# The decay of one state in eight moved to POOL, y copies moved to ACT, and transfers reordered in a scan kernel

## The chip, the cores and the metric

The kernel runs on one core of a Trainium2 chip. The metric is the device time of one execution in microseconds (us), the median of three runs. Engines: PE (TensorE, matmuls; PEld is its weight load), DVE (VectorE), ACT (ScalarE), POOL (GpSimd), SP (SyncE, which here only issues transfers; SPq is its queue). PSUM has eight banks of 128x512 f32, written by PE.

## The reference

Four residual layers on x of 64 batches, 64 steps and 256 features: two attention layers, then two state space layers. The change touches only the second pair:

```python
xr, gate = jnp.split(x @ W_in.T, 2, axis=-1)            # 512 each
xc = silu(conv4(xr + t_emb) + b_conv)                   # causal, 4 taps, each feature apart
xn = (xc - mu) / jnp.sqrt(var + 1e-05) * ln_g + ln_b
Bm, Cm, dt = jnp.split(xn @ W_xproj.T, 3, axis=-1)      # 16 states
dt = jnp.tanh(dt @ W_dt.T + b_dt) * 0.01
Ad = 1.0 + dt * A
Bd = Bm * jnp.minimum(norm(xn), 1.0)
def step(h, inputs):                                    # 64 steps
    ad, bd, xt, ct = inputs
    h = jnp.clip(h * ad[:, :, None] + bd[:, :, None] * xt[:, None, :], -10.0, 10.0)
    yt = jnp.einsum('bd,bdh->bh', ct, h)
    return (h, yt)
y = ys + D * xn
out = y * silu(gate) @ W_out.T
```

## The kernel before

64 batches are G = 8 groups of 8 batches. A state tile of a group is 128 partitions (8 batches x 16 states) by 512 features. Every engine has its program written out by hand; what orders them is semaphores alone, and each engine and SP's queue keep to the order of their program. A loop over two layers holds for each layer three stages.

**Front.** For each group in turn: input projection and convolution, normalisation, B, C and decay, and x split in three bf16 parts (xh, xmi, xlo; POOL makes xlo, `last_parts`). SP stores all of it to HBM: `store_x` (z, the normalised x), `store_gate` (sg), `store_scan`, which is `store_decay` (C and decay), `store_b` and `store_parts`. DVE may write the next group's z (`centred`) only when the store of the last has landed. After group 4's stores would be due, SP loads the tables of pass 0 (`load_tables`: Ub from nine loads, Cc and At from four each). The last group's small work is spread over the first 24 steps of the scan (`last_group`).

**Scan.** Two passes of four groups (QW = 4, index w), each 64 steps, in CHUNKS of CH = 4 steps; two chunks (h = 0, 1) make one round of the loop over c2. For each step and each w:

- PE writes the input term into PSUM bank w (`inputs`, Uw and the x block xq; a row of Uw holds the constant 10);
- DVE makes q = min(R, 20) - PSUM (L1744); q has two buffers by the step's parity;
- ACT makes R = relu(decay * q + 10) (`clamp`, L897), so that R of a step feeds q of the next: this is the chain of the recurrence;
- PE multiplies q by Wy and the x block by By (`y_of`) and collects y of a chunk in PSUM bank 4 + h.

When a chunk's y is full, DVE copies it to ys (`keep_y`, L1750) and SP stores it. POOL stages a chunk ahead (`stage`): four Uw, one for each w, when PE has used the old ones of that h; the decays Ast when ACT has used them; By and Wy when PE has. All eight x steps that fit into xq are refilled by SP (`load_x`, three loads for two steps), one block for each `y_done`. The tables of pass 1 are loaded at c2 = 6 of pass 0, and POOL waits for them (`tab_in[1]`) before it stages pass 1. At the start, xq's blocks 2 and 3 are loaded after group 6's `store_scan`.

**Post.** For each group PE turns y (L1360), DVE adds D*x and multiplies by the gate (yf, yg), PE multiplies by W_out (L1371, 16 matmuls), DVE adds to X (L1792). yt, xnp and sgp have two buffers; SP loads group g+2 when yg of group g is done, first the two gate tensors (`load_gate`, 2 x 1 MB), then y (`load_y`, two loads of 512 KB). PE's turn waits for all four.

## Time and profile before

| | us |
|---|---|
| runs | 1912.21, 1914.29, 1915.49 |
| median | 1914.29 |
| the profiled execution | 1915.77 |
| its span | 1912.7 |

| stretch of the span | what runs |
|---|---|
| 0 to 563 | attention |
| 563 to 797, 1241 to 1467 | front of each layer |
| 797 to 1155, 1467 to 1823 | scan of each layer |
| 1155 to 1241, 1823 to 1909 | post of each layer |

Over the span PE is busy for 1754.8 us, DVE 1646.0, ACT 1305.5, POOL 642.0. These are means over stages with different limits; how long a stage takes is read from the engine that does not wait in it. In a timeline a row is a run of equal instructions: its start, the time to the end of the last, their number, and in brackets the idle time before with what ended it. The instructions of a run overlap a little, so the pitch of one is the difference of starts by their number, not the mean duration.

### The profile page before, as it was taken

The numbers are of one execution on the slowest core, as the hardware profiler recorded it, in microseconds if no ns is written. First come the engines' busy times: TensorE is split into PE (matmuls) and PEld (weight loads), VectorE is DVE, ScalarE is ACT, GpSimd is POOL, SyncE is SP. The second block draws the span as 40 slices with busy tenths as digits, with TensorE's granted clock in tenths as the row PEclk, the third lists the DMA queues.
The fourth block names the chain that finished last, engine by engine and source line by source line (L and its number), as shares of the span: only waits on it lengthen the run. The fifth ranks groups of instructions, "written<-read, shape, count | busy, mean of one in ns | idle before, by whom it ended". The sixth has DMA issues, their size and how long they took to land.

```text
span 1912.7 us, 46171 instructions
## 1 busy us (share of the span) xinstructions
PE 1754.8 (92%) x15152; PEld 823.4 (43%) x15152; DVE 1646.0 (86%) x2380; ACT 1305.5 (68%) x2166; POOL 642.0 (34%) x591
## 2 busy tenths in 40 slices
PE   7999999999989998789999998899987899899978
PEld 5556566565544554322222224445553222222244
DVE  4788888888877997989999996579989899999965
ACT  3555446464637887789989990068877899899900
POOL 0223133232331111536656540001115466565400
PEclk9999999999999999899989999999998999999999
DMA  3000000000002434545445657624345454456577
GB/s 154 2 1 0 1 2 29 2 1 0 2 1 81 161 120 146 184 139 160 151 135 187 210 160 222 192 79 147 133 147 181 142 159 151 139 183 216 157 225 271
DMA packets 127179, 228.29 MB, mean 119 GB/s; under 512 B 36084, under 2 KB 61812, under 8 KB 118004
## 3 DMA queue, kind: packets, MB, share of 16 engines
q1 hardware_dynamic: 127064, 226.80, 36.0%
q8 instruction: 66, 1.08, 0.2%
q14 instruction: 49, 0.40, 0.1%
HBM read 143.40 MB, written 83.36 MB: 119 GB/s over the span
## 4 chain that ended last, share of the span: by engine, by line
PE 58%; DVE 17%; ACT 10%; issue 7%; DMA 5%; SPq 3%; DVEq 1%; POOL 0%; ACTq 0%; POOLq 0%
PE PS L912 14%; PE PS L1321 9%; PE PS L1304 8%; PE PS L1140 7%; ACT R L897 6%; DVE acc L1598 5%; DVE q L1744 4%; PE PS L978 4%; DMA yt<-y_d 3%; PE PS L1371 2%; PE PS L962 2%; PE PS L989 2%; PE PS L1324 2%; PE PS L937 2%; PE PS L972 1%
## 5 line engine op out<-in xcount | busy, mean ns | idle before, releaser
L897 ACT ACTIVATE R<-q,Ast 128x512 f32<-128x512 f32 x1024 | 637.9, 709 | 48.9 <-DVE q L1744 31.0
L1744 DVE SCALAR_TENSOR_TENSOR q<-R,PS 128x512 f32<-128x512 f32 x1008 | 610.2, 677 | 22.5 <-ACT R L897 11.8
L550 POOL TENSOR_TENSOR Uw<-Ub,rowmask 96x512 bf16<-96x512 bf16 x256 | 339.0, 1357 | 193.3 <-PE PS L1304 180.6
L1304 PE MATMUL PS<-xq,Uw 97*128 97x512 bf16 x1024 | 328.1, 398 | 54.7 <-DVE q L1744 39.1
L1321 PE MATMUL PS<-q,Wy 128*32 128x512 f32 x2016 | 284.3, 618 | 0.8 <-DVE q L1744 0.7
L1140 PE MATMUL PS<-X,Win 128*128 (+1 forms) x512 | 242.2, 614 | 5.7 <-DVEq L1577 2.9
L1304 PEld LDWEIGHTS PS<-xq,Uw 97*128 97x128 bf16 x1024 | 86.2, 98 | 371.2 <-DVE q L1744 318.2
L541 POOL TENSOR_TENSOR xlo<-xr,xmi 128x512 bf16<-128x512 f32 x64 | 73.3, 1167 | 457.4 <-ACT xmi L796 457.4
L912 PE MATMUL PS<-xn,Wl 128*128 128x512 f32 x384 | 183.7, 609 | 0.0
L507 POOL TENSOR_TENSOR ex<-ex,rs 128x1024 f32<-128x1024 f32 x32 | 78.5, 2453 | 201.4 <-DVE rs L1446 201.4
L1598 DVE SCALAR_TENSOR_TENSOR acc<-xp,Wc,acc 128x512 f32<-128x512 f32 x192 | 138.7, 780 | 0.5
L1140 PEld LDWEIGHTS PS<-X,Win 128*128 128x128 f32 x512 | 93.6, 194 | 105.6 <-issue 103.3
L654 ACT ACTIVATE pT<-PS 128x512 f32<-128x512 f32 x128 | 73.7, 596 | 95.3 <-PE PS L978 95.3
L1371 PE MATMUL PS<-yg,Wo 128*128 128x512 f32 x256 | 114.2, 601 | 0.0
L1324 PE MATMUL PS<-xq,By 96*32 96x512 bf16 x1024 | 112.3, 390 | 0.0
L1433 DVE TENSOR_REDUCE mx<-PS 128x32 f32<-128x2048 f32 x32 | 73.2, 2287 | 28.4 <-PE PS L962 28.4
L912 PEld LDWEIGHTS PS<-xn,Wl 128*128 128x128 f32 x384 | 67.2, 192 | 59.2 <-issue 54.6
L606 ACT ACT_TABLE_LOAD x18 | 23.1, 1283 | 98.3 <-DVE X L1792 90.0
L500 POOL TENSOR_TENSOR vsc<-vTd,vs_t 128x1024 f32<-128x1024 f32 x16 | 41.1, 2571 | 142.2 <-ACT vTd L646 142.2
L646 ACT ACTIVATE vTd<-PS 128x1024 f32<-128x1024 f32 x32 | 32.7, 1023 | 74.7 <-PE PS L912 74.7
L978 PE MATMUL PS<-ident,ex 128*128 128x128 f32 x512 | 77.6, 285 | 4.6 <-DVE ex L1450 3.0
L1443 DVE TENSOR_REDUCE sm<-ex 128x32 f32<-128x2048 f32 x32 | 73.1, 2283 | 9.5 <-ACT ex L658 9.5
(147 smaller groups left out, 2671.0 us busy)
## 6 DMA issues: line engine op xcount, KB each, us to landing
xq<-xpart_d SPq DMA_DIRECT2D x384, 192.0 KB
sg_d<-sg SPq DMA_DIRECT2D x16, 1024.0 KB, 4.0
xn_d<-z SPq DMA_DIRECT2D x16, 1024.0 KB, 4.1
y_d<-ys SPq DMA_DIRECT2D x64, 256.0 KB, 3.8
xnp<-xn_d SPq DMA_DIRECT2D x16, 1024.0 KB, 5.4
sgp<-sg_d SPq DMA_DIRECT2D x16, 1024.0 KB, 7.8
yt<-y_d SPq DMA_DIRECT2D x32, 512.0 KB, 9.6
xpart_d<-xh SPq DMA_DIRECT2D x16, 512.0 KB, 2.9
```

The lines of the kernel that those rows point to most:

```text
L507: pl.tensor_tensor(late_half(ex, r), late_half(ex, r), rs[:, r, :].rearrange("p (j e) -> p j e", j=4)[:, :, 4:8] .unsqueeze(3).broadcast_t ...
L550: pl.tensor_tensor(Uw[0:XROWS, h, w, :, :, :], Ub[0:XROWS, w, 0:N, ds(s0, CH)].rearrange("p n t -> p t n").unsqueeze(2).broadcast_to([XROW ...
L897: act.activation(R[:, w, :], q[:, t % 2, w, :], ACT.Relu, scale=Ast[:, h, w, t:t + 1], bias=CLIP).then_inc(ac_r, 1)
L912: mm = pe.matmul(PS[:, bank, :], Wl[l][:, w, c, m * P:(m + 1) * P], rhs[:, c, :], start=(c == 0), stop=(c == HC - 1))
L978: mm = pe.transpose(PS[:, turn_bank[k], j * P:(j + 1) * P], ex[:, k // 4, j, (k % 4) * P:(k % 4 + 1) * P], ident[:, :])
L1140: mm = pe.matmul(PS[:, m % DC, :], Win[:, c, m * P:(m + 1) * P], X[:, ds(g, 1), c, :].rearrange("p a t -> p (a t)"), start=(c == 0), stop= ...
L1304: pe.matmul(PS[:, w, :], Uw[0:KROWS, h, w, t, :, :].rearrange("p b n -> p (b n)"), xq[0:KROWS, hb, w, s8 % XT, :], start=True, stop=True). ...
L1321: pe.matmul(PS[32 * w:32 * w + 32, 4 + h, :], Wy[:, h, w, t * 32:(t + 1) * 32], R[:, w, :] if last else q[:, s8 % 2, w, :], start=(t == 0) ...
L1324: mm = pe.matmul(PS[32 * w:32 * w + 32, 4 + h, :], By[0:XROWS, h, t, w, MID - t * GB:MID + (CH - t) * GB], xq[0:XROWS, hb, w, xt, :], star ...
L1371: mm = pe.matmul(PS[:, 4 + 2 * u + m, :], Wo[:, c, m * P:(m + 1) * P], yg[:, u, c, :], start=(c == 0), stop=(c == DC - 1))
L1598: v.scalar_tensor_tensor(out=tiled(acc[:, m, :]), in0=xp[:, m, :, j:j + S], scalar=Wc[:, m, j:j + 1], in1=tiled(acc[:, m, :]), op0=ALU.mul ...
L1744: v.scalar_tensor_tensor(out=q[:, s8 % 2, w, :], in0=R[:, w, :], scalar=2 * CLIP, in1=PS[:, w, :], op0=ALU.min, op1=ALU.subtract).then_inc ...
```

## The change

1. **Decay of w = 3 on POOL at even steps.** In each chunk, at t = 0 and t = 2, R of w = 3 is made by POOL (`decayed`) as max(decay * q, -10), without the constant 10. For the step after it (odd) the constant row of Uw for w = 3 is 0 (one more memset before the first layer), and DVE takes min(R, 10) there. ACT makes 14 of the 16 R of a chunk, POOL two.
2. **y copies on ACT.** `keep_y` moves from DVE to ACT, after its three R of t = 2.
3. **POOL's staging** is cut in halves, `first_half` (Uw of w 0 and 1, Ast) and `second_half` (Uw of w 2 and 3, By, Wy), with one `decayed` between two halves. Each Uw piece waits for its own predecessor, and PE's step t = 0 waits for each piece by itself instead of for all four. The x parts of the last group are made one at a time. Pass 0 is written out instead of looped.
4. **SP in the front.** The z and gate stores of the fifth group (index 4) go ahead of the table loads; these are issued in four pieces between the stores of groups 4 and 5. The x blocks 2 and 3 of the scan are loaded ahead of `store_b` and `store_parts` of group 6. `store_parts` of the last group moves two steps later.
5. **SP in the post stage.** y of group g+2 is loaded when group g has been turned, ahead of the wait for yg and of the gate loads.

```diff
                     for w in range(QW):
+                        if t == 0:
+                            pe.wait_ge(pl_u, cn * QW + w + 1)
                         pe.wait_ge(dv_q, pi * (QW * S) + n * QW + w + 1)
...
+                        pooled = s8 % 2 == 1 and w == LAST
+                        if pooled:
+                            v.wait_ge(pr_r, pi * (S // 2) + (c2 * 4 + s8 // 2) + 1)
...
-                        v.scalar_tensor_tensor(out=q[:, s8 % 2, w, :], in0=R[:, w, :], scalar=2 * CLIP, in1=PS[:, w, :],
+                        v.scalar_tensor_tensor(out=q[:, s8 % 2, w, :], in0=R[:, w, :], scalar=CLIP if pooled else 2 * CLIP, in1=PS[:, w, :],
...
-                            for w in range(QW):
+                            for w in range(QW - (t + 1) % 2):
                                 act.wait_ge(dv_q, cn * (QW * CH) + QW * t + w + 1 + QW)
...
+                            if t == 2 and (h or before):
+                                keep_y(pi, c2 * 2 + h - 1, 1 - h)
...
+                def decayed(ps, c2, h, t):
+                    cn = chunk_no(ps, c2, h)
+                    pl.wait_ge(pl_a, cn + 1)
+                    pl.wait_ge(dv_q, cn * (QW * CH) + QW * t + LAST + 1 + QW)
+                    alone(pl)
+                    pl.tensor_scalar(R[:, LAST, :], q[:, t % 2, LAST, :], Ast[:, h, LAST, t:t + 1], -CLIP, ALU.mult, ALU.max).then_inc(pr_r, 1)
...
+                for c2 in range(CHUNKS // 2):
+                    more = c2 + 1 < CHUNKS // 2
+                    nxt = (0, c2 + 1) if more else (1, 0)
+                    decayed(0, c2, 0, 0)
+                    if c2:
+                        second_half(0, c2, 1)
...
+                    decayed(0, c2, 0, 2)
...
+                    if not more:
+                        pl.wait_ge(tab_in[1], l * (16 * TABLES) + 16 * TABLES)
+                        alone(pl)
+                    first_half(*nxt, 0)
+                    decayed(0, c2, 1, 0)
+                    second_half(*nxt, 0)
...
+                    decayed(0, c2, 1, 2)
...
+                    first_half(*nxt, 1)
```

How it moves the rows. First SP in the front, around the fifth group of a layer. Before, the tables stand ahead of that group's stores (the loop over groups 4 and 5 begins behind them):

```order
L356 REGISTER_ALU x2
L367 DMA Ub<-bpart_d 8x4x1088 x9
L373 DMA Cc<-cc_d 128x1x64 x4
L373 DMA At<-a_d 128x1x64 x4
L406 UNCONDITIONAL_BRANCH
L406 ISA
L319 ISA
L319 DMA xn_d<-z 128x2048
L314 ISA
L315 ISA
L315 DMA sg_d<-sg 128x2048
```

Now:

```order
L323 ISA
L324 DMA xn_d<-z 128x2048
L319 ISA
L320 DMA sg_d<-sg 128x2048
L361 REGISTER_ALU x3
L372 DMA Ub<-bpart_d 8x4x1088 x3
L328 DMA cc_d<-Cn 4x32x64 x2
L328 DMA a_d<-am 4x32x64 x2
L372 DMA Ub<-bpart_d 8x4x1088 x3
L328 DMA bpart_d<-tvp 4x32x64 x6
L349 DMA xpart_d<-xh 128x4x512
L349 DMA xpart_d<-xmi 128x4x512
```

The store of z (xn_d) and of the gate went ahead of the tables, and the nine loads of Ub stand in threes between the groups' other stores.

POOL at the first chunks. Before, a chunk is staged in one piece, here the first chunk and the start of the second:

```order
L550 TENSOR_TENSOR Uw<-Ub,rowmask 96x512 x4
L554 REGISTER_ALU
L556 COPY Ast<-At 128x16
L557 ISA
L559 TENSOR_TENSOR By<-Ub,rowmask 96x16x8
L563 TENSOR_TENSOR Wy<-Cc,masks 128x4x4x8
L547 ISA
L550 TENSOR_TENSOR Uw<-Ub,rowmask 96x512 x4
L554 REGISTER_ALU
L556 COPY Ast<-At 128x16
```

Now, in the scan's first rounds, from the R of w = 3 at t = 0 of a second chunk (TENSOR_SCALAR) through the half with By and Wy and the next R to the following half:

```order
L597 TENSOR_SCALAR R<-q,Ast 128x512
L567 REGISTER_ALU
L568 TENSOR_TENSOR Uw<-Ub,rowmask 96x512
L567 REGISTER_ALU
L568 TENSOR_TENSOR Uw<-Ub,rowmask 96x512
L582 ISA
L584 TENSOR_TENSOR By<-Ub,rowmask 96x16x8
L588 TENSOR_TENSOR Wy<-Cc,masks 128x4x4x8
L597 TENSOR_SCALAR R<-q,Ast 128x512
L567 ISA
L568 TENSOR_TENSOR Uw<-Ub,rowmask 96x512
L567 REGISTER_ALU
```

Two Uw with By and Wy, or two Uw with Ast, stand between two R; whatever a half waits for, the next R is queued behind.

SP in the post stage, half of a round of its loop. Before:

```order
L396 ISA
L396 DMA xnp<-xn_d 128x2048
L397 DMA sgp<-sg_d 128x2048
L392 ISA
L392 DMA yt<-y_d 64x4x512
L392 ISA
L392 DMA yt<-y_d 64x4x512
```

Now:

```order
L397 ISA
L397 DMA yt<-y_d 64x4x512
L397 ISA
L397 DMA yt<-y_d 64x4x512
L401 ISA
L401 DMA xnp<-xn_d 128x2048
L402 DMA sgp<-sg_d 128x2048
```

The two loads of yt went ahead of the two of the gate, and ahead of the wait for yg.

## Rows read from the trace of the kernel before

**Rows 1.** Windows: busy us per engine, clock, DMA share, GB/s; scan, pass 1.

```profile
996.20:1151.00 154.80, 147.75 (x980) 39.14 (x978) 154.80 (x259) 151.06 (x245) 85.95 (x98) 1.00 0.58 183
```

**Rows 2.** Timeline of DVE in the scan: start us, us, instructions.

```profile
1006.33 9.64 DVE L1744 SCALAR_TENSOR_TENSOR q<-R,PS 128x512 f32<-128x512 f32 x16
1015.89 0.68 DVE L1750 COPY ys<-PS 128x512 f32<-128x512 f32 x1
1016.49 9.64 DVE L1744 SCALAR_TENSOR_TENSOR q<-R,PS 128x512 f32<-128x512 f32 x16
```

**Rows 3.** Timeline of ACT in the scan, one chunk.

```profile
1608.06 9.91 ACT L897 ACTIVATE R<-q,Ast 128x512 f32<-128x512 f32 x16 [0.25 <-DVE q L1744]
```

**Rows 4.** Timeline of PE's weight loads in the scan.

```profile
1003.47 0.10 PEld L1304 LDWEIGHTS PS<-xq,Uw 97*128 97x128 bf16 x1 [0.50 <-DVE q L1744]
```

**Rows 5.** Groups of POOL's instructions: busy us, mean ns, idle before; one memset.

```profile
L550 POOL TENSOR_TENSOR Uw<-Ub,rowmask 96x512 bf16<-96x512 bf16 x256 | 339.0, 1357 | 193.3 <-PE PS L1304 180.6 <-DMA At<-a_d 12.7
...
L541 POOL TENSOR_TENSOR xlo<-xr,xmi 128x512 bf16<-128x512 f32 x64 | 73.3, 1167 | 457.4 <-ACT xmi L796 457.4
...
L563 POOL TENSOR_TENSOR Wy<-Cc,masks 128x128 f32<-128x128 f32 x64 | 26.6, 416 | 0.0
L559 POOL TENSOR_TENSOR By<-Ub,rowmask 96x128 bf16<-96x128 bf16 x64 | 26.4, 412 | 98.6 <-PE PS L1324 98.6
...
L556 POOL COPY Ast<-At 128x16 f32 (+1 forms) x64 | 15.0, 234 | 1.3 <-ACT R L897 1.3
...
570.52 0.95 POOL L528 MEMSET Wy<- 128x1024 f32 x1
```

**Rows 6.** Timelines near the end of pass 0: SP's issue, POOL, DVE.

```profile
967.53 2.48 SPq L373 DMA_DIRECT2D At<-a_d  x4
...
972.18 5.24 POOL L550 TENSOR_TENSOR Uw<-Ub,rowmask 96x512 bf16<-96x512 bf16 x4 [6.40 <-DMA At<-a_d]
...
947.41 0.68 DVE L1750 COPY ys<-PS 128x512 f32<-128x512 f32 x1
```

**Rows 7.** SP's timeline in the front, and DVE's wait in both layers.

```profile
715.57 6.63 SPq L367 DMA_DIRECT2D Ub<-bpart_d  x9
...
727.68 0.36 SPq L319 DMA_DIRECT2D xn_d<-z  x1
...
DVE z L1604 <- DMA xn_d<-z: 11.8, 2, 5.9
```

**Rows 8.** Timelines of DVE in two groups and of POOL beside the second.

```profile
747.87 6.83 DVE L1598 SCALAR_TENSOR_TENSOR acc<-xp,Wc,acc 128x512 f32<-128x512 f32 x10
...
776.70 8.70 DVE L1598 SCALAR_TENSOR_TENSOR acc<-xp,Wc,acc 128x512 f32<-128x512 f32 x10
...
766.36 5.36 POOL L550 TENSOR_TENSOR Uw<-Ub,rowmask 96x512 bf16<-96x512 bf16 x4
```

**Rows 9.** Timelines at the start of each scan: PE in both layers, SP.

```profile
812.00 1.89 PE L1304 MATMUL PS<-xq,Uw 97*128 97x512 bf16 x4 [3.35 <-DMA xq<-xpart_d]
...
1482.02 1.03 PE L1304 MATMUL PS<-xq,Uw 97*128 97x512 bf16 x4 [3.09 <-POOL Uw L550]
...
793.91 1.30 SPq L323 DMA_DIRECT2D a_d<-am  x2
...
802.97 1.11 SPq L377 DMA_DIRECT2D xq<-in_ones  x1
```

**Rows 10.** After the scan: wait in both layers, PE's last turn, three windows.

```profile
PE PS L1360 <- DMA yt<-y_d: 19.2, 8, 6.1
...
1224.85 1.97 PE L1360 MATMUL PS<-ident,yt 128*128 128x128 f32 x16 [1.38 <-DMA yt<-y_d]
...
1182.00:1190.00 8.00, 8.00 (x32) 4.38 (x31) 3.95 (x6) 0.00 (x0) 0.00 (x0) 1.00 1.03 346
...
1201.00:1211.00 10.00, 7.84 (x31) 4.22 (x30) 6.54 (x10) 0.00 (x0) 0.00 (x0) 1.00 1.04 324
1211.00:1225.00 14.00, 12.01 (x41) 5.83 (x40) 8.39 (x11) 0.00 (x0) 0.00 (x0) 1.00 0.88 264
```

More of the change, by code:

```diff
@@ L585, in _ @@
-                pl.wait_ge(sg_st, l * (16 * G) + 16 * G + 16)
-                pl.wait_ge(xf_st, l * (16 * G) + 16 * G + 16)
-                alone(pl)
-                pl.memset(words(pass_tables[1][0]), 0.0).then_inc(tab_zero, 1)
-                with pl.Fori(6, CHUNKS // 2) as c2:
-                    for h in range(2):
-                        stage(0, c2, h)
-                pl.wait_ge(tab_in[1], l * (16 * TABLES) + 16 * TABLES)
-                alone(pl)
-                with pl.Fori(0, CHUNKS // 2) as c2:
-                    for h in range(2):
-                        stage(1, c2, h)
+                    first_half(0, 0, h)
@@ new lines, in _ @@
+                    second_half(0, 0, h)
+                for k in range(TT):
+                    last_part(l * G + G - 2, k)
+                last = l * G + G - 1
+                for c2 in range(CHUNKS // 2):
[4 more added lines that the diff above has]
+                        second_half(0, c2, 1)
+                    if c2 == 3:
+                        last_part(last, 2)
+                    decayed(0, c2, 0, 2)
+                    if c2 == 3:
+                        last_part(last, 3)
+                    if not more:
[4 more added lines that the diff above has]
+                    second_half(*nxt, 0)
+                    if c2 == 2:
+                        last_part(last, 0)
+                    decayed(0, c2, 1, 2)
+                    if c2 == 2:
+                        last_part(last, 1)
+                    if c2 == 4:
+                        pl.wait_ge(xlo_r, l * (G * TT) + G * TT)
+                        pl.wait_ge(xq_st, l * (G * 48) + G * 48 + 48)
+                        pl.wait_ge(sg_st, l * (16 * G) + 16 * G + 16)
+                        pl.wait_ge(xf_st, l * (16 * G) + 16 * G + 16)
+                        alone(pl)
+                        pl.memset(words(pass_tables[1][0]), 0.0).then_inc(tab_zero, 1)
+                    first_half(*nxt, 1)
@@ L884, in last_group, with keep_y, clamp @@
                         middle_part(it, 3)
-                def clamp(pi, c2, first, between=None):
+                def keep_y(pi, ck, h):
+                    act.wait_ge(pe_yq, pi * (2 * S) + ck * (2 * CH) + 2 * CH + USED)
+                    act.wait_ge(y_out[h], pi * (CHUNKS // 2 * 16) + (ck - h) * 8 + 16)
+                    act.activation(ys[:, h, :], PS[:, 4 + h, :], ACT.Copy).then_inc(dv_y, 1)
+                def clamp(pi, c2, first, before, between=None):
                     for h in range(2):
@@ L894, in clamp @@
                                 between(c2 * 8 + h * CH + t)
-                            for w in range(QW):
+                            for w in range(QW - (t + 1) % 2):
                                 act.wait_ge(dv_q, cn * (QW * CH) + QW * t + w + 1 + QW)
```

131 lines of the change are left out of this document (78 added, 53 removed).

## The prediction

> **What bounds the kernel now.** I read the stretches first, then each engine in order of time inside them. In the steady scan VectorE (DVE) is busy for the whole stretch, 154.80 of 154.80 us [rows 1]; the time of a chunk is DVE's. Inside it [rows 2], 16 q instructions start at 1006.33 and the y copy at 1015.89: 9.56 us for 16, so 0.5975 each (the 0.68 of a row is longer than the pitch, since instructions overlap). The copy takes 0.60 more: 1016.49 - 1006.33 = 10.16 us for four steps. The others have room. ScalarE (ACT) needs 9.91 us for its 16 R and then sits idle for 0.25 [rows 3]: pitch (9.91 - 0.71)/15 = 0.613. TensorE (PE) waits 0.50 us in the step for DVE's fourth q [rows 4]. POOL's staging is 4 x 1.357 + 0.234 + 0.412 + 0.416 = 6.49 us of each 10.16 [rows 5]. Outside the scan three places are bound by a transfer, and each is touched by the new order: [rows 7], [rows 9], [rows 10].
>
> **The steady scan: -30.0.** The copy leaves DVE. Per layer there are 32 copies: 5 in the first 24 steps, 10 in the rest of pass 0, 1 early in pass 1 beside other idle time, 15 in the rest of pass 1, 1 at the end. 25 lie in the steady part, so 2 x 25 x 0.60 = 30.0, if nobody else is late. ACT gives two R of a chunk and takes one copy of the same shape, which I count like an R: 15 x 0.613 = 9.2 under 9.56 [rows 3]. The tightest pair of steps has seven R and the copy, 4.9 against 4.78, made good in the next pair, which has seven. PE runs at this pace already within each run of 16 q, still waiting for DVE [rows 4].
>
> POOL decides. Its new instruction (one SBUF input of 128x512 f32, a per-partition scalar, multiply and max) has no row; call it D. Below it stands a POOL memset, 0.95 us for 1024 elements, 0.47 for 512, which reads nothing; above it a subtraction of 128x512 with two inputs, 1.167 [rows 5]. I take 0.7, between them, nearer the one with fewer reads. Latency: D may start after q of w=3 and its result is wanted when DVE has done three more q, 3 x 0.5975 = 1.79 later; with about 0.1 to start and to release, D up to 1.6 fits. Throughput: 2D + 6.49 <= 9.56 gives D <= 1.53. In the half with two Uw, By and Wy, D queues behind 2 x 1.357 + 0.83 = 3.54 of the 4.78 between two D; what it is late may be taken from the 1.79: 2D <= 4.78 + 1.79 - 3.54, D <= 1.51. So any D between the two bounds costs nothing; the staging that it is moved past is due over two us later. The same holds for single release of pieces: PE gets w=0 earlier, where it never waits now.
>
> The Trainium skill (GPSIMD Engine Reference, section 3.1) gives bodies of at most two operations 1.03 cycles an element, an estimate of 0.44 us plus dispatch; no run here shows it, and by it the sum is the same.
>
> **First 24 steps: -3.** Five copies go, the first beside idle time: 4 x 0.60 x 2 = 4.8. POOL's share rises here and DVE's small two-input instructions of the last group can be caught behind it (next part); I take off 0.9 a layer.
>
> **Front: -9.8.** SyncE (SP) now issues 17 table loads (nine for B, four for C, four for the decays) in a row from 715.57, and only at 727.68 the store of z, which DVE awaits for 5.9 us in each layer, 11.8 together [rows 7]. The new order puts that store ahead of the tables. Nothing takes its place: the later table loads go behind each group's stores, and the last eight (about 5 us of issue) end some 8 us before the staging that they release would be late. But they do delay it: POOL's first staging, begun at 766.36 now [rows 8], starts about 775 in a schedule that is 5.9 earlier. Staging costs DVE time where DVE reads two SBUF tensors: ten conv steps take 8.70 beside it and 6.83 without [rows 8]; with the smaller cases the group loses about 3.7 us. Afterwards it meets the chain of small normalisation instructions instead, five with two SBUF inputs. I take one us more than now per layer: 11.8 - 2.0.
>
> The trace shows that DVE waits for POOL instructions there and that q, with one input in PSUM, keeps its pitch beside POOL. The Trainium skill (SBUF — State Buffer, "Who interferes with whom") says so: two SBUF inputs contend with a GpSimd instruction that reads SBUF, one does not; the lock is for the whole instruction. By it D leaves q alone. It speaks against the new place of the staging: five small instructions each behind one Uw.
>
> By rows that rival is 5 x 1.34 = 6.7 against 3.7 now, 3 us a layer instead of my 1, a sum 4 us worse.
>
> **First input blocks: -6.5.** PE waits 3.35 and 3.09 us at step 4 of each layer; the second is put down to POOL, whose pieces had long been staged, so it is the same transfer [rows 9]. SP comes to it at 802.97, after the b and x parts of group 6 and a wait for tvp. They now go behind, so that the load follows the decay store, which ends at 795.2: 7.7 us sooner. I count the two waits; four matmuls after them take 1.89 instead of 1.03 for some steps, which may give two us more.
>
> **A new wait in pass 0: +5.6.** POOL's wait for the tables of pass 1 stood with nothing urgent behind it: 6.40 us of idle [rows 6]. Now D of step 60 is queued behind it. SP issues that block without a gap, so its landing is tied to step 50: 972.18 - 947.41 = 24.8 us. At 2.39 a step, step 60's q ends at 23.9 and D's result is wanted at 25.7. POOL gets it out at 24.8 + 2 x 1.34 + 0.2 + 0.1 + 0.7 = 28.5: 2.8 late, twice. Bounds 1 and 4 each.
>
> **After the scan: -13.** PE stands for y and gate loads for 19.2 us in both layers [rows 10]. y now goes first, 4 us before the gates. But PE waits for both, and the 16 DMA engines are full (shares 1.03 and 1.04 at 346 and 324 GB/s). Six groups of 3.15 MB at the mean, 335 GB/s, need 56.4 us; from about 1161.5, when the last y store can have landed, that ends at 1217.9, where the last turn now begins at 1224.85: 6.5 a layer, 13. Without the bandwidth limit it would be about 20; if the gates land no sooner, 4.
>
> **Sum.** 30.0 + 3 + 9.8 + 6.5 - 5.6 + 13 = 56.7. The profiled execution took 1915.8 (span 1912.7, 3.1 around it), so 1859.1; the median of the runs is 1914.3, 1.5 lower: **1858**. Bounds of the terms: 27 to 30, 0 to 6, 4 to 12, 3 to 8.5, -8 to -2, 4 to 20, together 1842 to 1884.
>
> **Rivals.**
> (a) The y loads bring little, the gates being last anyway: 13 becomes 2 to 4, time 1868. For: full DMA engines. Against: a gap in their work after 1211 (share 0.88) that an earlier issue fills. 14%.
> (b) D takes 1.5 to 2.0. Then POOL sets the chunk, 2D + 6.5: at 1.8 it is 10.1, 27 of the 30 are gone, time 1885. 8%.
> (c) Slower: POOL's arithmetic with two operations and a scalar operand takes over 2.1 us. 27 us come from elsewhere, so the chunk must exceed 9.56 + 57/50 = 10.7. At D = 2.45 it is 11.4: 50 x 1.84 = 92 more, 1950. Nothing in the trace has such a rate (2.3 ns an element is the worst), but nothing shows the instruction. 6%.
> (d) The change does not do what it says: the moved loads make another queue late in the front, and one wait replaces the other. 1870. 4%.
>
> **Numbers.** Forecast 68%, own range 1846 to 1870; the rest as above. The range for 8 in 10 is 1842 to 1884. Under 0.2% (4 us) a measurement can't tell a change. Faster 92%, same 2%, slower 6%.
>
> **What would show it.** DVE's q in unbroken runs across chunks at a pitch of 0.60, a chunk of 9.56, no idle time on POOL's R but for one wait of two to three us near the end of each pass 0; D near 0.7; the z store before the tables and no 5.9 us of DVE idle; no transfer wait at step 4; turns of y with waits below two us and full DMA engines between. Wrong if D exceeds 1.5, if POOL's waits for PE or ACT hold a D back in every chunk, or if the first staging stretches DVE's small instructions to over 1.3 us each.

## The result and the profile of the changed kernel

The changed kernel takes 1945.6 us (median; 1937.7 to 1952.9) against 1913.3 for the kernel before on the same chip: ratio 1.017, 95% interval 1.012 to 1.022. It is slower by 32 us, where 1858 was forecast. The profiled execution took 1941.0, its span 1938.8.

The stages, read from starts in DVE's timeline (first z of the front, first q of the scan, the clamp at the end of a pass, last X of the post), us, layer 1 / layer 2:

| stage | before | changed | difference of both | forecast |
|---|---|---|---|---|
| front (z to q) | 206.0 / 205.4 | 201.8 / 203.0 | -6.7 | -9.8 |
| pass 0 | 183.7 / 183.1 | 192.6 / 192.6 | +18.4 | pass 0 and 1: -33.9 |
| pass 1 | 170.1 / 168.9 | 182.5 / 182.2 | +25.8 | |
| post (clamp to X) | 89.6 / 89.0 | 84.7 / 83.3 | -10.6 | -13 |

What lies between differs by 1 us. So front and post came within 3 us of the forecast here, and the scan missed it by 78 us.

Two of POOL's groups (busy us, mean ns of one, idle before them), and ACT's y copies; the first two answer to [rows 5]:

```profile
L568 POOL TENSOR_TENSOR Uw<-Ub,rowmask 96x512 bf16<-96x512 bf16 x256 | 339.9, 1348 | 37.4 <-DMA At<-a_d 28.4
...
L597 POOL TENSOR_SCALAR R<-q,Ast 128x512 f32<-128x512 f32 x128 | 255.3, 1994 | 96.2 <-DVE q L1825 46.7 <-issue 26.8 <-PE PS L1401 11.1
...
L958 ACT ACTIVATE ys<-PS 128x512 f32<-128x512 f32 x64 | 36.8, 575 | 4.3 <-PE PS L1401 4.3
```

L597 is the new instruction, D: **1.99 us** (128 of them, 1.992 to 2.100), where I took 0.7 and let it reach 1.17. Its 255 us account for the growth of POOL's busy time, 642.0 to 895.0; the staging costs what it did.

DVE in pass 1 (answers to [rows 2]); the times in brackets are idle time and what ended it:

```profile
1033.81 0.69 DVE L1825 SCALAR_TENSOR_TENSOR q<-R,PS 128x512 f32<-128x512 f32 x1 [0.64 <-POOL R L597]
1034.74 4.28 DVE L1825 SCALAR_TENSOR_TENSOR q<-R,PS 128x512 f32<-128x512 f32 x7 [0.24 <-issue]
1039.46 5.02 DVE L1825 SCALAR_TENSOR_TENSOR q<-R,PS 128x512 f32<-128x512 f32 x8 [0.44 <-POOL R L597]
...
1055.85 0.69 DVE L1825 SCALAR_TENSOR_TENSOR q<-R,PS 128x512 f32<-128x512 f32 x1 [0.62 <-POOL R L597]
```

DVE stops at each q of w = 3 in an odd step, and POOL's R ends each stop. From 1033.81 to 1055.85 are two chunks, four pairs of steps of 5.65, 5.53, 5.32 and 5.54 us: 11.02 a chunk, where it was 10.16. POOL in the same pass, a little later:

```profile
1059.47 2.00 POOL L597 TENSOR_SCALAR R<-q,Ast 128x512 f32<-128x512 f32 x1 [0.79 <-DVE q L1825]
1061.54 2.64 POOL L568 TENSOR_TENSOR Uw<-Ub,rowmask 96x512 bf16<-96x512 bf16 x2
1064.15 0.40 POOL L584 TENSOR_TENSOR By<-Ub,rowmask 96x128 bf16<-96x128 bf16 x1
1064.50 0.40 POOL L588 TENSOR_TENSOR Wy<-Cc,masks 128x128 f32<-128x128 f32 x1
1065.00 1.99 POOL L597 TENSOR_SCALAR R<-q,Ast 128x512 f32<-128x512 f32 x1
1067.08 2.64 POOL L568 TENSOR_TENSOR Uw<-Ub,rowmask 96x512 bf16<-96x512 bf16 x2
1069.66 0.20 POOL L577 COPY Ast<-At 128x16 f32 x1
1070.32 1.99 POOL L597 TENSOR_SCALAR R<-q,Ast 128x512 f32<-128x512 f32 x1 [0.46 <-DVE q L1825]
```

Two kinds of step pairs alternate. Between 1059.47 and 1065.00 POOL has no idle time: D, two Uw, By and Wy take 5.53 us for a pair of steps, in which DVE has 4.78 of work. Between 1065.00 and 1070.32 (5.32) POOL waits for DVE (0.46): here it is latency, five q from the one that waited to the one that D reads, then D, then the next q. Once in eight steps, behind the last q of a round of its loop over c2, DVE is idle for 0.24 more and waits for nothing that the profile shows (row 1034.74); that makes the longest pair. ACT is no longer near the bound: it sits idle for 0.38 to 0.45 in the same pairs.

### The profile page after: what moved, and what is told of

Same layout as the page of the kernel before. It is cut to its first block and busy times, and to the rows that moved or that the text cites. A ratio compares the mean times of both kernels' runs of the same rounds, so it can differ in the third digit from the quotient of the medians.

```text
span 1938.8 us, 46236 instructions
## 1 busy us (share of the span) xinstructions
PE 1739.6 (90%) x15152; PEld 815.6 (42%) x15152; DVE 1628.1 (84%) x2316; ACT 1276.8 (66%) x2102; POOL 895.0 (46%) x720
## 5 line engine op out<-in xcount | busy, mean ns | idle before, releaser
L1825 DVE SCALAR_TENSOR_TENSOR q<-R,PS 128x512 f32<-128x512 f32 x1008 | 620.3, 683 | 88.2 <-POOL R L597 63.2
L971 ACT ACTIVATE R<-q,Ast 128x512 f32<-128x512 f32 x896 | 579.5, 712 | 121.9 <-DVE q L1825 100.0
L1381 PE MATMUL PS<-xq,Uw 97*128 97x512 bf16 x1024 | 321.4, 395 | 105.8 <-DVE q L1825 96.9
L597 POOL TENSOR_SCALAR R<-q,Ast 128x512 f32<-128x512 f32 x128 | 255.3, 1994 | 96.2 <-DVE q L1825 46.7
L1381 PEld LDWEIGHTS PS<-xq,Uw 97*128 97x128 bf16 x1024 | 82.1, 97 | 420.0 <-DVE q L1825 379.2
L524 POOL TENSOR_TENSOR ex<-ex,rs 128x1024 f32<-128x1024 f32 x32 | 78.5, 2453 | 201.4 <-DVE rs L1523 201.4
```

The lines of the kernel that those rows point to most:

```text
L524: pl.tensor_tensor(late_half(ex, r), late_half(ex, r), rs[:, r, :].rearrange("p (j e) -> p j e", j=4)[:, :, 4:8] .unsqueeze(3).broadcast_t ...
L597: pl.tensor_scalar(R[:, LAST, :], q[:, t % 2, LAST, :], Ast[:, h, LAST, t:t + 1], -CLIP, ALU.mult, ALU.max).then_inc(pr_r, 1)
L971: act.activation(R[:, w, :], q[:, t % 2, w, :], ACT.Relu, scale=Ast[:, h, w, t:t + 1], bias=CLIP).then_inc(ac_r, 1)
L1381: pe.matmul(PS[:, w, :], Uw[0:KROWS, h, w, t, :, :].rearrange("p b n -> p (b n)"), xq[0:KROWS, hb, w, s8 % XT, :], start=True, stop=True). ...
L1825: v.scalar_tensor_tensor(out=q[:, s8 % 2, w, :], in0=R[:, w, :], scalar=CLIP if pooled else 2 * CLIP, in1=PS[:, w, :], op0=ALU.min, op1=AL ...
```

## Experiments

"The changed kernel" is the one measured above. A chunk's time is read as above, between equal rows of DVE in pass 1. The kernels ran on three chips, so each ratio is to the kernel before on the same chip, whose median was 1912.1, 1915.9 or 1914.4 us; times of kernels from two chips can differ by some 4 us for that alone.

### How much the transfers gave

The kernel before with SP's two new orders (items 4 and 5 of the change, no others).

> The kernel before with SP's two new orders alone (front and post); POOL makes no R, the y copies stay on DVE. Theory 1 (what the changed kernel loses, it loses by POOL's R of 1.99 us, and the transfers gave what its trace shows): front 4.1 + 2.8 us shorter, the two waits at step 4 (3.35 and 3.09) gone, post 4.9 + 5.7 shorter, together 24: 1889 us, steady chunk 10.16 as before. Theory 2 (the post gains only because the scan before it ends late or the y copies moved): post at most 4 shorter in both layers, 1896. Slower than 1905 would say that the transfers are part of the loss.

Measured: 1898.7 us (1897.8 to 1901.4), ratio 0.992 (0.990 to 0.994). The chunk is 10.17, as before. Front 200.2 / 203.4, pass 0 180.6 / 180.6, post 86.9 / 88.5. So the transfers are a gain of 13 us, not a part of the loss; the first steps gave most of what the two waits of [rows 9] held (pass 0 3.2 and 2.5 shorter, of 3.35 and 3.09), the front 5.8 and 2.0, the post only 2.7 and 0.5. That is theory 2's limit of 4 us for the post, 7 below theory 1's 10.6, and most of the 10 by which the expected total was missed.

Then the front order alone; the post keeps gates before y (the edit is against the kernel just measured):

```diff
                     for u in range(2):
-                        sp.wait_ge(po_mm, (l * G + g2 * 2 + u) * DC + DC)
-                        load_y(g2 * 2 + u + 2, u)
                         sp.wait_ge(yg_r, (l * G + g2 * 2 + u) * DC + DC)
                         load_gate(g2 * 2 + u + 2, u)
+                        load_y(g2 * 2 + u + 2, u)
```

> The kernel before with SP's new order in the front and at the first x blocks alone; the post stage loads as before (gates, then y). Theory 1 (of the transfers' 13.4 us the trace puts some 8 to 11 in front and first steps, and 3 in the post): 1903 to 1905, post 89 per layer as before. Theory 2 (the y order is worth what was forecast, 6.5 a layer, and was only disturbed in that run): 1911. Theory 3 (the y order costs as much as it gains): 1898.

Measured: 1902.5 (1895.5 to 1910.6), ratio 0.995 (0.993 to 0.997); post 90.3 / 86.5. The intervals of the two overlap, so what the y order is worth can't be told by the totals: 3.8 us between medians, but only 1.5 when each is taken from the kernel before on its own chip (11.9 against 13.4 saved). The stage itself says a little more, since eleven profiled kernels have the new order unaltered: 83.3 to 89.9, mean of their 22 stages 86.9, against 88.9 for the four stages of this kernel and the one before. That is 2 us a layer, with a spread of 3 either way (the next part shows what goes with it).

### What bounds the post

Transfers as changed, and for the six later groups one quarter of sg (the rest of the gating is left out):

```diff
-                        load_gate(g2 * 2 + u + 2, u)
+                        sp.dma_start(xnp[:, u, :, :], xn_d[ds(g2 * 2 + u + 2, 1)].rearrange("a p c t -> p (a c) t")).then_inc(po_in[u], 16)
+                        sp.dma_start(sgp[:, u, 0:1, :], sg_d[ds(g2 * 2 + u + 2, 1), :, 0:1, :]
+                                     .rearrange("a p c t -> p (a c) t")).then_inc(po_in[u], 16)
```

> Transfers as changed, POOL, ACT and DVE as before, and in the post stage only one quarter of the gate tensor sg is loaded for the six later groups (256 KB instead of 1 MB; the other quarters keep old values, so that part of the gating is left out). Theory 1 (the loads are bound by the rate of the DMA engines; what lands last is sg): 2.4 instead of 3.1 MB a group, at 320 GB/s 7.4 us, under the 8.6 that PE and DVE need; PE's waits of 1 to 2 us at each turn go, post 78 to 80 a layer instead of 87. Theory 2 (bound by the chain of issue and landing of the first tensor, whatever the size): at most 2 shorter.

Measured: 1876.7 (one run), post 76.6 / 76.5, below the 78 to 80 of theory 1. PE's turns in this kernel:

```profile
1159.47 1.96 PE L1373 MATMUL PS<-ident,yt 128*128 128x128 f32 x16 [0.30 <-DMA sgp<-sg_d]
1168.14 1.91 PE L1373 MATMUL PS<-ident,yt 128*128 128x128 f32 x16
```

And in the one with whole gates (the two new orders alone), one turn of layer 1 and one of layer 2:

```profile
1160.81 1.96 PE L1372 MATMUL PS<-ident,yt 128*128 128x128 f32 x16 [1.72 <-DMA sgp<-sg_d]
...
1856.55 3.63 PE L1372 MATMUL PS<-ident,yt 128*128 128x128 f32 x16 [2.67 <-DMA sgp<-sg_d]
```

A window of the kernel with one quarter of sg (busy us of PE, PEld, DVE, ACT, POOL, clock, DMA share, GB/s):

```profile
1160.00:1215.00 55.00, 55.00 (x199) 29.73 (x197) 40.28 (x55) 0.00 (x0) 0.00 (x0) 1.00 0.71 207
```

With fewer bytes PE never stops (55.00 of 55.00 us, DMA share 0.71) and a group takes 8.6; with all bytes each of the six later turns of layer 1 waits 1.0 to 2.4 for sgp. The stage is bound by the transfers, and which tensor is last goes with the order: y in [rows 10], sgp now. In the changed kernel the DMA queue moved 19.1 MB between 1171 and 1235, 298 GB/s at a share of 95%, where I had taken 335 at a full share. The kernel before, over its loads of the post stage in layer 1 (the same columns), and one of its turns there with the granted clock beside it:

```profile
1160.00:1225.00 65.00, 54.25 (x184) 29.05 (x183) 41.61 (x57) 0.00 (x0) 0.00 (x0) 0.95 0.92 291
...
1174.42 3.67 PE L1360 MATMUL PS<-ident,yt 128*128 128x128 f32 x16 [5.88 <-DMA yt<-y_d]
...
1174.00:1178.00 4.00, 3.58 (x17) 3.58 (x18) 2.36 (x4) 0.00 (x0) 0.00 (x0) 0.50 1.01 426
```

It moved 291 GB/s there already; my 335 was the mean of two short windows of [rows 10], and the third, with 264, was left out. Over 1160 to 1215 the kernel with whole gates shows 282 GB/s at a share of 0.89, so the engines are not quite full either. How much of the waits is their rate, and how much that the gate loads are issued only after yg, these runs don't separate.

The last two rows show one more price of these waits. After PE had waited 5.88 us, the turn ran at a granted clock of 0.50 (1.2 GHz) and took 3.67 us instead of 1.96. In the new order the waits are shorter, but some turns are still slow, up to 3.6 us: the one at 1856.55 above, with 0.50 from 1857 to 1860, comes after a wait of 2.67. The slow ones follow waits of 1.92 to 4.60 us; after 2.35 and 2.46 others are not slow. This divides the 22 stages with the new order: the 12 in which one of the six later turns is slow take 87.3 to 89.9 us, the 10 without one 83.3 to 86.9. The changed kernel has none in either layer, the kernel before one in each. No experiment changed the clock alone.

### Is it POOL's R?

The changed kernel with all sixteen R on ACT; copies, halves, unrolled pass and transfers stay:

```diff
-        ACT_TWO = 2 * QW - 1
+        ACT_TWO = 2 * QW
...
-                        pooled = s8 % 2 == 1 and w == LAST
+                        pooled = False
...
-                            for w in range(QW - (t + 1) % 2):
+                            for w in range(QW):
```

> The changed kernel with all sixteen R of a chunk on ACT again (constant 10 in every step); y copies on ACT, staging in halves and transfers as changed. Theory 1 (POOL's R sets the chunk of 11.0): the chunk becomes ACT's 17 x 0.613 = 10.42 us, 0.26 above the kernel before over 50 chunks (13 us), less some 3 us in the first 24 steps; with the transfers' 24 us off, 1899. DVE waits for ACT, not for POOL. Theory 2 (the y copies on ACT, the halves or the unrolled pass cost it): the chunk stays above 10.8 and the time above 1930.

Measured: 1905.2 (1900.4 to 1913.6), ratio 0.996 (0.994 to 0.998); chunk 10.29:

```profile
1034.28 9.84 DVE L1821 SCALAR_TENSOR_TENSOR q<-R,PS 128x512 f32<-128x512 f32 x16 [0.42 <-ACT R L967]
...
1054.85 9.83 DVE L1821 SCALAR_TENSOR_TENSOR q<-R,PS 128x512 f32<-128x512 f32 x16 [0.43 <-ACT R L967]
```

ACT's row of this kernel shows the copy's real price: 16 R from 1023.08 to the copy at 1032.88 are 0.6125 each, and the next R starts 0.48 after the copy, at 1033.36.

```profile
1023.08 9.92 ACT L967 ACTIVATE R<-q,Ast 128x512 f32<-128x512 f32 x16
1032.88 0.60 ACT L954 ACTIVATE ys<-PS 128x512 f32<-128x512 f32 x1
1033.36 9.92 ACT L967 ACTIVATE R<-q,Ast 128x512 f32<-128x512 f32 x16
```

16 x 0.6125 + 0.48 = 10.28, the chunk. (1899 was expected; the front's last group, 34.3 in both layers, and the post, 88.9 and 87.5, stayed longer.) So the slowness comes with POOL's R, as theory 1 said: the copies, the halves and the unrolled pass are all still there. And ACT with the copy but without help is slower than DVE with it (10.29 against 10.16).

Then the copies back on DVE, two R on POOL:

```diff
-                            if t == 2 and (h or before):
-                                keep_y(pi, c2 * 2 + h - 1, 1 - h)
...
                         step(pi, c2, s8, first)
+                        if s8 == 2 and before:
+                            keep_y(pi, c2 * 2 - 1, 1)
+                        if s8 == 6:
+                            keep_y(pi, c2 * 2, 0)
```

> The changed kernel with the y copies back on DVE (at steps 2 and 6, as before); two R on POOL and all else as changed. Theory 1 (with D = 1.99 DVE waits for POOL in each pair of steps, and the copy falls into that wait): steady chunk 11.0 to 11.2 as with the copies on ACT, total within 6 us of the changed kernel's. Theory 2 (the copy's 0.60 adds to the wait): chunk 11.6, 1970.

Measured: 1949.6 (1947.4 to 1952.2), ratio 1.019 (1.016 to 1.022), the same as the changed kernel's.

```profile
1026.75 3.08 DVE L1817 SCALAR_TENSOR_TENSOR q<-R,PS 128x512 f32<-128x512 f32 x5 [0.44 <-POOL R L597]
1029.75 0.68 DVE L1823 COPY ys<-PS 128x512 f32<-128x512 f32 x1
1030.35 2.62 DVE L1817 SCALAR_TENSOR_TENSOR q<-R,PS 128x512 f32<-128x512 f32 x4
...
1048.80 3.08 DVE L1817 SCALAR_TENSOR_TENSOR q<-R,PS 128x512 f32<-128x512 f32 x5 [0.44 <-POOL R L597]
```

(1048.80 - 1026.75) / 2 = 11.03. The copies fall into time in which DVE would wait anyway: moving them off DVE, for which the 30 us stood in the sum, gained nothing at this D.

### Why is D 1.99?

Three kernels, each with another form of the one instruction and everything else as changed (one operation; scalar by value; product). The first and the third leave out the lower bound of -10, the second puts 0.99 in place of the decay:

```diff
-pl.tensor_scalar(R[:, LAST, :], q[:, t % 2, LAST, :], Ast[:, h, LAST, t:t + 1], -CLIP, ALU.mult, ALU.max).then_inc(pr_r, 1)
+pl.tensor_scalar(R[:, LAST, :], q[:, t % 2, LAST, :], Ast[:, h, LAST, t:t + 1], None, ALU.mult).then_inc(pr_r, 1)
+pl.tensor_scalar(R[:, LAST, :], q[:, t % 2, LAST, :], 0.99, -CLIP, ALU.mult, ALU.max).then_inc(pr_r, 1)
+pl.tensor_tensor(R[:, LAST, :], q[:, t % 2, LAST, :], Ast[:, h, LAST, t:t + 1].broadcast_to([P, 512]), ALU.mult).then_inc(pr_r, 1)
```

> The changed kernel with POOL's R as one operation with the same scalar pointer (decay x q); the lower bound of -10 is left out. If each of the two operations costs its share, D is about 1.0 to 1.2; if the form with a scalar has one rate whatever it computes, D stays 1.99. Time 1870 to 1885 in the first case, 1940 in the second.

> The changed kernel with POOL's R as 0.99 x q and the lower bound, both scalars given by value instead of the decay read from Ast (the decay of w = 3 at even steps is left out). It asks whether the read of a scalar per partition makes the 1.99. If so, D falls to 1.1 to 1.3 and the time below 1890; if the form with two operations and scalars has its rate wherever they come from, D stays 1.99 and the time 1940.

> The changed kernel with POOL's R as one product of two tensors (q and the decay repeated along the row), without the lower bound of -10, which is left out: it asks what the form with two operations and a scalar costs. Theory A (a product costs what the subtraction xlo costs, 1.17 us): D 1.17 to 1.2, inside the room of three q; POOL 2 x 1.25 + 6.25 = 8.8 a chunk; DVE runs unbroken at 0.5975, chunk 9.56 to 9.7, and the total is near what was forecast for the whole change; with the transfers' 13 (instead of 29) and the copies' place: 1866 to 1880. Theory B (the read or the f32 output sets the rate): D stays 1.9 to 2.0, 1940.

The group of the instruction (busy us, mean ns of one, idle before) with one operation:

```profile
L597 POOL TENSOR_SCALAR R<-q,Ast 128x512 f32<-128x512 f32 x128 | 200.8, 1569 | 100.6 <-DVE q L1825 52.8 <-issue 30.8 <-PE PS L1401 11.4
```

With the scalar by value:

```profile
L597 POOL TENSOR_SCALAR R<-q 128x512 f32<-128x512 f32 x128 | 245.8, 1920 | 96.1 <-DVE q L1825 46.3 <-issue 27.1 <-PE PS L1401 11.9
```

As a product:

```profile
L597 POOL TENSOR_TENSOR R<-q,Ast 128x512 f32<-128x512 f32 x128 | 133.0, 1039 | 144.9 <-DVE q L1825 80.6 <-issue 48.3 <-PE PS L1401 10.6
```

DVE in pass 1 of the product form (the row is cut off by the end of the view):

```profile
1035.62 31.00 DVE L1825 SCALAR_TENSOR_TENSOR q<-R,PS 128x512 f32<-128x512 f32 x51 [0.39 <-PE PS L1381]
```

| form | D (median) | chunk | time | runs |
|---|---|---|---|---|
| two operations, scalar from Ast | 1.99 | 11.02 | 1945.6 | 4 |
| two operations, scalar by value | 1.92 | 10.85 | 1934.0 | 1 |
| one operation, scalar from Ast | 1.57 | 9.98 | 1888.8 | 1 |
| product of two tensors | 1.04 | 9.7 | 1874.5 (1867.7 to 1878.8) | 4 |

So the read of the decay costs 0.07, the second operation 0.43, and the form with scalars by itself, even with one operation, half as much again as a product with two tensor inputs (of which the second repeats one value along the row; the subtraction with two whole inputs, 1.167, is below it too). The 1.57 lies between the two values expected for one operation, so neither of its theories holds; the form by value went as its second, the product as theory A. That the form with fewer reads is the slower one is the opposite of what I assumed when I leaned to the memset. Why the form with a scalar is slow no run shows. The forecast's other terms can now be seen at nearly the pace that they were made for. The ratio of the product form is 0.979 (0.975 to 0.982), and its scans take 676.9 us against 705.8 before and 750.0 in the changed kernel. Of the 78 us by which the scan missed the forecast, 73 come back with this one instruction.

DVE near the end of pass 0 in the product form:

```profile
963.63 3.08 DVE L1825 SCALAR_TENSOR_TENSOR q<-R,PS 128x512 f32<-128x512 f32 x5 [1.96 <-POOL R L597]
967.40 2.48 DVE L1825 SCALAR_TENSOR_TENSOR q<-R,PS 128x512 f32<-128x512 f32 x4 [0.70 <-PE PS L1381]
```

POOL at the same place:

```profile
959.85 2.62 POOL L568 TENSOR_TENSOR Uw<-Ub,rowmask 96x512 bf16<-96x512 bf16 x2 [3.60 <-PE PS L1381]
...
962.56 1.03 POOL L597 TENSOR_TENSOR R<-q,Ast 128x512 f32<-128x512 f32 x1
```

SP's last issue of that block of tables:

```profile
955.67 2.48 SPq L378 DMA_DIRECT2D At<-a_d  x4
```

This is the new wait for the tables of pass 1: POOL idle for 3.60 before the staging, D behind it (the profile names a matmul of PE as the releaser; POOL waits there for the tables and for PE, and PE had run on without a stop), DVE late by 1.96. The loads of the decays are issued until 958.15 and the wait ends 1.7 after that. I had put 2.8, bounds 1 and 4. In the changed kernel the same wait of POOL is 0.61 and DVE's stop there the usual 0.65, because POOL comes late by itself: one price hid the other.

### Latency or load?

If two bounds alternate, taking one away leaves the other. In the changed kernel, w = 3 is taken before w = 2 in every even step by PE, DVE and ACT, so that five q lie between the q that D reads and the one that wants its R, instead of three:

```diff
+        turn_of = lambda t: (0, 1, 3, 2) if t % 2 == 0 else (0, 1, 2, 3)
...
-                    for w in range(QW):
+                    for pos, w in enumerate(turn_of(s8 % CH)):
```

> The changed kernel with w = 3 taken before w = 2 in every even step (t = 0 and 2), nothing else. It takes latency away and leaves POOL's load. Theory 1 (both bind in turn: 5.31 by latency, 5.53 by load): the latency half goes, the load stays, 2 x (1.99 + 0.08) + 5.25 + 0.2 + 0.8 = 10.4 to 10.6 a chunk instead of 11.0, time 1912 to 1925. Theory 2 (latency alone): 9.6 to 9.9, below 1880. Theory 3 (load alone): 11.0 and 1940 stay.

Measured: 1934.4 (1928.7 to 1936.3), ratio 1.010 (1.007 to 1.013), 9 above the end of theory 1's range.

```profile
1032.07 0.69 DVE L1826 SCALAR_TENSOR_TENSOR q<-R,PS 128x512 f32<-128x512 f32 x1 [0.47 <-POOL R L598]
...
1042.65 10.03 DVE L1826 SCALAR_TENSOR_TENSOR q<-R,PS 128x512 f32<-128x512 f32 x16 [0.32 <-POOL R L598]
1053.12 0.69 DVE L1826 SCALAR_TENSOR_TENSOR q<-R,PS 128x512 f32<-128x512 f32 x1 [0.44 <-POOL R L598]
```

(1053.12 - 1032.07) / 2 = 10.53, inside the 10.4 to 10.6 of theory 1. Without the latency the load is left. The time misses by what lies outside the scan: the scans are 18 us shorter than the changed kernel's (732.1 against 750.0), the post 8.5 longer (176.5 against 168.0), as that stage varies (a later turn is slow in both layers here, in none of the changed kernel's).

Now the other way: one R of sixteen on POOL (t = 0), the staging of the next chunk whole behind it, so that the load fits and the latency stays.

```diff
-                            for w in range(QW - (t + 1) % 2):
+                            for w in range(QW - (t == 0)):
...
-                        pooled = s8 % 2 == 1 and w == LAST
+                        pooled = s8 % CH == 1 and w == LAST
...
+                with pl.Fori(0, CHUNKS // 2 - 1) as c2:
+                    decayed(1, c2, 0)
+                    stage(1, c2, 1)
+                    decayed(1, c2, 1)
+                    stage(1, c2 + 1, 0)
```

> One of sixteen R of a chunk on POOL (w = 3 at t = 0) and fifteen on ACT, then the whole staging of the next chunk behind it; y copies on ACT, transfers as changed. Theory 1 (latency of 1.99 us against three q of DVE, and POOL's sum): POOL has 1.99 + 6.49 = 8.5 us of work in a chunk, so only the latency stays: DVE idles 0.44 once a chunk, 9.56 + 0.44 = 10.0, against 9.81 for ACT's 16; 0.16 below the kernel before over 50 chunks, 8 us, and 3 in the first steps: 1878. Theory 2 (a hand-over from and to POOL costs more than its duration, whatever the load): idle of 0.8 or more each, chunk 10.4, 1900.

Measured: 1904.6 (1904.5 to 1908.4), ratio 0.996 (0.994 to 0.998); a miss of 27 us.

```profile
1039.85 9.71 DVE L1799 SCALAR_TENSOR_TENSOR q<-R,PS 128x512 f32<-128x512 f32 x16 [0.44 <-POOL R L592]
1050.00 9.80 DVE L1799 SCALAR_TENSOR_TENSOR q<-R,PS 128x512 f32<-128x512 f32 x16 [0.44 <-POOL R L592]
1060.24 1.88 DVE L1799 SCALAR_TENSOR_TENSOR q<-R,PS 128x512 f32<-128x512 f32 x3 [0.44 <-POOL R L592]
```

The idle time is the 0.44 expected, but the chunk is 10.15 and 10.24. Start to start the late q costs 1.12 instead of 0.60, which is 0.52; and one q in the next step comes 0.15 late in the longer of the two, after PE. PE had waited for the late q and still has the 8 matmuls of q and Wy to do in that step; that this keeps it from making the time up is a reading, not tested. A stop of 0.44 costs 0.59 to 0.68. The rest of the miss is in the transfers (1898.7, where 1889 was the base) and in the last group of the front.

### A kernel that beats both

One R on POOL, w = 3 before w = 2 at t = 0 only, and ACT's copy of y in the gap that the missing R leaves there, one chunk later; SP stores it accordingly.

```diff
+        turn_of = lambda t: (0, 1, 3, 2) if t == 0 else (0, 1, 2, 3)
...
-                            if t == 2 and (h or before):
-                                keep_y(pi, c2 * 2 + h - 1, 1 - h)
+                                if t == 0 and w == 1 and before:
+                                    keep_y(pi, c2 * 2 + h - 2, h)
```

> One R of sixteen on POOL as in the run with one per chunk (chunk 10.19 there), but at t = 0 every engine takes w = 3 before w = 2, so that five q of DVE instead of three lie between the q that POOL reads and the q that wants its R; and the y copy of ACT stands in the gap that the missing R leaves at t = 0, one chunk later than before (two chunks after its own). Transfers as changed. Theory 1 (the loss of a lone R is latency, 2.06 needed against 1.79): room becomes 2.39 + 0.6 = 2.99 from start to start against 0.68 + 0.08 + 1.99 + 0.06 = 2.8, POOL has 8.4 us of work in a chunk, DVE idles for nobody, chunk 9.6 to 9.7 (ACT: 15 x 0.613 + 0.48 = 9.68); 50 x 0.5 below the transfers alone (1898.7): 1872 to 1878. Theory 2 (a hand-over to POOL costs whatever the room, or ACT falls behind): idle of 0.3 or more a chunk stays, 1890 to 1900.

Measured: 1891.6 (1885.9 to 1896.6), ratio 0.987 (0.984 to 0.990), 14 above theory 1's range. The waits for POOL are gone, but the chunk is 9.97, not 9.65:

```profile
1040.36 19.77 DVE L1802 SCALAR_TENSOR_TENSOR q<-R,PS 128x512 f32<-128x512 f32 x32 [0.16 <-PE PS L1357]
1060.29 1.88 DVE L1802 SCALAR_TENSOR_TENSOR q<-R,PS 128x512 f32<-128x512 f32 x3 [0.16 <-PE PS L1357]
```

32 q take 19.93. Each pair of steps holds one late q (0.77 to 0.84 after the last instead of 0.60), put down to PE; ACT is busy for 59.91 of 60 us there and PE for 56.90. Theory 2's "or ACT falls behind" fits that, its hand-over cost does not; which of the two engines holds the last 0.3 us is open.

Last, the same with the staging of the second chunk moved from the front behind POOL's first R:

```diff
-                for h in range(2):
-                    stage(0, 0, h)
+                stage(0, 0, 0)
...
                     decayed(0, c2, 0)
-                    if c2:
-                        stage(0, c2, 1)
+                    stage(0, c2, 1)
```

> The kernel with one R on POOL and w = 3 ahead of w = 2 at t = 0 (1891.6, front 201.8 and 203.2 us from the first z to the first q), with the staging of the second chunk moved behind POOL's first R, so that one chunk's staging instead of two stands beside the front's last group. Theory 1 (the front lost 3 to 4 us a layer to DVE instructions with two SBUF inputs that wait behind Uw): the last group's 34.3 to 35.5 us from z to z becomes 31 or less, front 3 to 4 shorter a layer; part of it may be given back in the first steps; 1884 to 1888. Theory 2 (it is something else that makes this group long): unchanged, 1891.

Measured: 1882.9 (1880.0 to 1885.3), ratio 0.984 (0.982 to 0.987), the fastest of the kernels here that compute everything. The front is 197.2 / 197.0, read as in the table, where the kernel that it was made from has 203.0 / 203.6, and its last group takes 29.6 and 29.5 instead of 35.3 and 35.4. That is 12 us for both layers, more than the 8.7 between the medians, which come from two chips. DVE's normalisation chain in the kernel that it was made from, beside POOL's staging ([rows 8] show the same with the convolution):

```profile
778.30 1.36 DVE L1450 SCALAR_TENSOR_TENSOR n<-n,mn 128x128 f32<-128x128 f32 x1
779.70 1.32 DVE L1452 SCALAR_TENSOR_TENSOR n<-n,mn 128x128 f32<-128x128 f32 x1
...
783.71 2.00 DVE L1690 TENSOR_TENSOR mr<-mn,rc 128x128 f32<-128x128 f32 x1
```

And in the kernel with late staging:

```profile
779.94 0.27 DVE L1448 SCALAR_TENSOR_TENSOR n<-n,mn 128x128 f32<-128x128 f32 x1
780.24 0.29 DVE L1450 SCALAR_TENSOR_TENSOR n<-n,mn 128x128 f32<-128x128 f32 x1
...
781.22 0.29 DVE L1688 TENSOR_TENSOR mr<-mn,rc 128x128 f32<-128x128 f32 x1
```

Five instructions take 7.44 us in the one and 1.69 in the other (first start to the next start after them), which is all of the 5.7 us by which the group is shorter. In the changed kernel the same five take 5.87.

## Why the prediction was wrong

**The step that failed** is the size of D in "The steady scan": "Call it D ... I take 0.7", between a memset of 0.47 and a subtraction of 1.167. It is 1.99. Both rows were of another kind: neither has a scalar, and neither a second operation. The upper end was taken from the nearest row that did more reads, as if reads set the rate; no row bounded the operations from above. Rival (c) named this very doubt and got 6%; it asked for a D over 2.1 for a loss. Its "2.3 ns an element is the worst" was a little low (POOL's product of 128x1024 in the attention layers takes 2571 ns on average, 2.5 an element), and D's 3.9 ns is above all of POOL's large instructions before.

The Trainium skill (GPSIMD Engine Reference, section 3.1) gives the rate from which the prediction's estimate of 0.44 us for the body comes. Every form with a scalar here is far above it (1.57 to 1.99), and the measurement decides. What it adds for dispatch doesn't fill the gap by the rows at hand: a POOL memset of one element takes 0.10 us.

**The price of a large D** was the second error. Rivals (b) and (c) used 2D + 6.5 alone: 10.47 at D = 1.99, which is 46 us over 50 chunks, 1904 in all, and still faster than before. The chunk is 11.02, 73 us over 50, because the two conditions don't average: the pair with By and Wy pays its load (5.53), the other pair pays latency (5.32), though it has load to spare, and one pair in four holds 0.24 more of DVE's idle time. The latency limit itself stood in the prediction (D up to 1.6); for D above it, it was forgotten. By it, 1.99 is 0.4 late in every pair, and the run with w = 3 ahead showed that share: 11.02 against 10.53. One more term was missing in pass 0. From the last xr to the clamp it takes 117.8 us in the changed kernel and 104.6 before, 13.2 more, where ten chunks of 11.02 would be 8.6 more. The four xlo pieces and a memset of Ub, which stood before nobody in the old order, now stand before a D: DVE's stops near them are 1.10, 1.55, 1.20 and 1.71 instead of 0.44 to 0.66. So the scan's miss of 78 adds up: 73 from the chunk, 4 from the rest of pass 0 (9.2 more, where 5.6 had been counted for the tables), 1.5 from the first steps.

```profile
882.22 4.87 DVE L1825 SCALAR_TENSOR_TENSOR q<-R,PS 128x512 f32<-128x512 f32 x8 [1.55 <-POOL R L597]
...
922.51 5.01 DVE L1825 SCALAR_TENSOR_TENSOR q<-R,PS 128x512 f32<-128x512 f32 x8 [1.71 <-POOL R L597]
928.05 4.87 DVE L1825 SCALAR_TENSOR_TENSOR q<-R,PS 128x512 f32<-128x512 f32 x8 [0.53 <-POOL R L597]
```

**Steady scan, -30.** Where D is small the copy does leave DVE, but the chunk became 9.7, not 9.56 (product form: from the first to the last of 51 q 31.00 - 0.68 us, 0.606 each, times 16): 23 of the 30. PE, of which I said that it "runs at this pace already", is busy for 58.37 of 60 us there and ends DVE's remaining stops; that it had used the gap at each copy to catch up is my reading. ACT's copy costs 0.48 to 0.57 where ACT doesn't wait after it, a little below the 0.613 that I took.

**First 24 steps and first blocks, -9.5 together.** Right: from the first q to the last xr of the last group 79.1 and 78.5 became 74.8 and 74.8, 8.0 less, of which the transfers alone gave 5.7, and the two transfer waits at step 4 are gone. DVE's idle time put down to POOL in this part is 1.3 us in layer 1.

**Front, -9.8.** The wait of 5.9 for the store of z [rows 7] is gone in both layers, as said. SP's rows in layer 1 of the changed kernel: the store, then the first tables.

```profile
711.58 0.35 SPq L324 DMA_DIRECT2D xn_d<-z  x1
...
718.33 2.68 SPq L372 DMA_DIRECT2D Ub<-bpart_d  x3
```

What takes the place of the wait is nearer the rival's "5 x 1.34" than my 1 us: the last group grew from 30.7 to 34.3, and the front is 4.2 and 2.5 shorter, 6.7 in all, where I had 9.8 and the rival 5.8. It is not one price: with the transfers alone, POOL's first staging starts 19.9 us after the z of the group before in both layers, and the last group takes 31.2 in one and 35.4 in the other; what decides that is open. The run with late staging gave 6 us a layer more.

By the Trainium skill (SBUF — State Buffer, "Who interferes with whom") an instruction of DVE with two SBUF inputs contends with a GpSimd instruction that reads SBUF, and one with at most one SBUF input doesn't. The rows above agree (7.44 us against 1.69), and q beside D keeps its 0.5975.

**Post, -13.** Mechanism partly right: y no longer lands last, SP issues it earlier. But the gates then do, and the transfers run at 298 GB/s, as they did before (291), not at 335. (By its own numbers the term was 1224.85 - 1217.9 = 7.0 a layer, not 6.5.) In the changed kernel it was -10.6, in an execution in which none of its later turns was slow; that was luck. Over all kernels with this order the mean is 4 in both layers. Rival (a), "the gates being last anyway", 2 to 4, is what stands.

**New wait for the tables, +5.6.** Right in its mechanism and size where the scan has the assumed pace (1.96 against 2.8), hidden in the changed kernel.

**Rivals.** (a) came true beside the main error. (b) had the right range for D and the wrong price (1885). (c) came out at the right time by luck (1950, measured 1945.6): it took D = 2.45, and its threshold of 2.1 was too high because its formula lacked the latency. (d) is excluded: each moved load stands where it should and the waits that it aimed at are gone.

With D inside the bounds that I gave it (1.04, lower bound left out), all this together gives 1874.5 (measured): inside the range and 16 above the forecast. By its stages the scan is 5 short of it, the front 3, the post 7, and 1 lies between. (The best ends of the terms add up to 74.5, so the low end of the range was 1840, not 1842.)

## What to carry to other kernels

An instruction form that no row of the trace shows has no upper bound from rows of other forms: until it is measured, take as its end the point at which it would turn the result, and give that a real chance. When work in a recurrence goes to a slower engine, compute its latency condition and its load condition for every pair of steps, add the larger of each pair, and look at what else is queued ahead of it on that engine. One R of sixteen moved off, with the y copies, lost 6 us against the transfers alone; with an order that gives the slow engine more room, and the copy in ACT's gap, the same gained some 7 to 11.
